# Reordering the gates at the end of a graph layer, with the residual base on VectorE

## Chip, core and metric

The kernel runs on one core of a Trainium2 chip. A core has TensorE (PE, matrix products into eight PSUM banks), VectorE (DVE), ScalarE (ACT), GpSimd (POOL) and SyncE (SP, which issues loads here). The metric is the device time of one execution in microseconds, the median of several.

## What is computed

Four layers are added one after another to x, 256 nodes by 512 features: a graph diffusion, a mixture of experts with feed-forward experts, a second graph layer, and a mixture of LSTM experts. The change is in the third, cut here to what matters (h is the normalised x):

```python
m = relu(concat(h[src], edge_attr) @ W1.T + b1) @ W2.T + b2
agg = segment_sum(m, dst)
i_r, i_z, i_n = split(agg @ W_ih.T + b_ih)
h_r, h_z, h_n = split(h @ W_hh.T + b_hh)
r, z = sigmoid(i_r + h_r), sigmoid(i_z + h_z)
n = tanh(i_n + r * h_n)
h_new = (1 - z) * n + z * h
x = x + h + gamma * (h_new - run_mean) * rsqrt(run_var + eps) + beta
```

There are 4352 edges, so the edge part is a loop of 34 tiles of 128 edges.

## The kernel before

The nodes are two tiles of 128 rows (n = 0, 1). A float32 product is made of three matmuls of split operands: `hi*hi + hi*lo + lo*hi`. Weights come in chunks of 512x512: SyncE loads one into `raw`, ScalarE rounds it to `whi` (L565), VectorE subtracts to `wlo` (L791). Each of the three engines has its own written order of instructions, and `cut_to(q)` in the orders of ScalarE and VectorE says up to which chunk the splits are to be done there. A split waits for the slot that it writes; a load waits for the VectorE split of the chunk four before it.

The order of the second graph layer: TensorE makes the first linear part, then the recurrent products of the reset gate (g = 0, banks 6 and 7) and of the update gate (g = 1, banks 2 and 3) for both tiles (`whh`). ScalarE copies all four to `gh` (`gh_copy`). Then the edge loop runs: GpSimd gathers rows (L541), TensorE makes the edge products (L1293 to L1295, into banks 2 to 5), VectorE adds (L1232, `mp`), ScalarE cuts (L757), VectorE splits (L1212, `m_lo`) and writes one-hot tiles (L1219), and TensorE sums by destination (L1641, L1643, banks 0 and 1). VectorE also splits the edge attributes for four tiles at a time (L1203, `ea_lo`). Behind its last gather GpSimd makes the base of the residual, x + g2b + xn, in place (L547 and L548, for both tiles), where g2b and g2s are the shift and scale of the batch normalisation.

After the loop: the recurrent products of the candidate (g = 2, banks 4 and 5), the aggregate through W2, its split, and the input products `Wih`. TensorE takes these tile by tile, in each the reset, update and candidate gate. VectorE's loop (L1257 on) goes tile by tile too: it adds the two parts of each gate (L1260), takes the sigmoids from ScalarE (L775), multiplies the reset gate in (L1266), builds the residual (L1270 to L1273), adds the candidate (L1276), takes the tanh (L777) and finishes x (L1279, L1280). `link(...)` marks an instruction whose successor on VectorE waits for its end by a semaphore; without it the next may start behind it.

Behind the layer come the layer norm of x (L808 to L818, its root on GpSimd, L471), the transposes of the normalised x on TensorE (L1322), the routing logits (L1407), the routing on VectorE (L944 to L972, among them the cast L951) and the LSTM experts. `keep_busy` (L1314) gives TensorE matmuls without use between two stages. While the logits are made, ScalarE copies the transposes (L584), cuts a chunk and writes two cuts more (L702, L705), and GpSimd subtracts for the low rows of the biases (L488).

Of the kernel before, what the change touches and what calls it, by code (L numbers as in the profile page):

```python
# [27 lines left out]
NT = T // P  # L28
D = 512
KB = D // P  # L30
# [8 lines left out]
SPL = 4  # L39
# [34 lines left out]
CHUNK = {key: n for n, key in enumerate(ORDER)}  # L74
# [13 lines left out]
def build(nc, A, out, node_rows):  # L88
    f32, f32r, bf16, i32, u32 = (mybir.dt.float32, mybir.dt.float32r, mybir.dt.bfloat16,
                                 mybir.dt.int32, mybir.dt.uint32)  # L90
    ALU = mybir.AluOpType
    ACT = mybir.ActivationFunctionType
# [3 lines left out]
    with ctx:  # L96
# [8 lines left out]
        whi = [sb(f"whi{i}", [P, KB, C], f32r) for i in range(SPL)]  # L105
        wlo = [sb(f"wlo{i}", [P, KB, C], f32r) for i in range(SPL)]
        x = sb("x", [P, NT, D])
        xn = sb("xn", [P, NT, D])
# [102 lines left out]
        with ExitStack() as st:  # L211
            g1_xT_hi = sb("g1_xT_hi", [P, NT, KB, P], f32r, st)
            g1_xT_lo = sb("g1_xT_lo", [P, NT, KB, P], f32r, st)
            A_sb = sb("A_sb", [P, NT, D], f32, st)
            gh = sb("gh", [P, NT, 3, D], f32, st)
# [4 lines left out]
            gsel = sb("gsel", [P, 3, P], f32r, st)  # L220
# [14 lines left out]
            with ExitStack() as st2:  # L235
# [5 lines left out]
                rz = sb("rz", [P, NT, 3, D], f32, st2)  # L241
# [3 lines left out]
            g2s = sb("g2s", [P, D], f32, st)  # L245
            g2b = sb("g2b", [P, D], f32, st)
# [7 lines left out]
        B = [ctx.enter_context(nc.psum_tensor(f"bank{i}", [P, C], f32)) for i in range(8)]  # L254
# [62 lines left out]
        def both_tiles(eng, n, first_tile, value, chunk):  # L317


            if n == 0:  # L320
                eng.wait_ge(first_tile, value)
            else:
                eng.wait_ge(chunk_used, chunk + 1)


        class Run:
# [61 lines left out]
            "a_ps", "a_sb", "a_out", "gh_ps", "gh_sb", "w1e_hi", "w1e_lo", "ea_hi", "ea_lo", "e_ps",  # L388
            "mp", "m_hi", "m_lo", "hot", "sum_ps", "s1_hi", "s1_lo", "agg_ps", "agg", "ag_hi", "ag_lo",
            "deg_d", "deg_ps", "ones", "warm",  # L390
            "gi_ps", "rz_in", "rz", "n_in", "n", "rows", "gsel", "x_base")}
        ea_in = [sem(f"g1_ea_in{i}") for i in range(3)]
        gath_in = [sem(f"g1_gath_in{i}") for i in range(GATH)]
        out_done = sem("out_done")
# [63 lines left out]
        def _(pool):  # L458
# [15 lines left out]
            bn_link = Chain(pool, pool_chain)  # L474
# [46 lines left out]
            for r in range(4):  # L521
# [7 lines left out]
                out=mp[:, SUMS - 1, :], out_offset=None, in_=A["x"],  # L529
# [12 lines left out]
                    out=gath[:, t % GATH, :], out_offset=None, in_=node_rows[:, :],  # L542
                    in_offset=bass.IndirectOffsetOnAxis(ap=src_i[:, t:t + 1], axis=0)).then_inc(gath_in[t % GATH], 16)


            for n in range(NT):
                bn_link(pool.tensor_tensor(x[:, n, :], x[:, n, :], g2b[:, :], ALU.add))  # L547
                pool.tensor_tensor(x[:, n, :], x[:, n, :], xn[:, n, :], ALU.add).then_inc(g1["x_base"], 1)  # L548

            root(3)  # L550
            moe_params(A["lstm_b"], A["L1_ffn_bo"])
# [4 lines left out]
        def _(act):  # L556
# [19 lines left out]
            def cut_to(n):  # L576
                while done[0] < n:
                    cut_hi(done[0])
                    done[0] += 1
# [164 lines left out]
            def gh_copy(g, n):  # L744
                both_tiles(act, n, g1["gh_ps"], g + 1, CHUNK[("gnn", "Whh", g)])
                act.activation(gh[:, n, g, :], B[(6, 2, 4)[g] + n][:, :], ACT.Copy).then_inc(g1["gh_sb"], 1)

            for g in range(2):
                for n in range(NT):
                    gh_copy(g, n)  # L750
                if g == 0:
                    cut_to(first + SPL + 1)
            for t in range(ET):
                act.wait_ge(g1["mp"], t + 1)
                if t >= MSG:
# [14 lines left out]
            cut_to(first + 2 * SPL)  # L770
            cut_to(first + 2 * SPL + 1)
            for n in range(NT):
                for g in range(2):
                    act.wait_ge(g1["rz_in"], 2 * n + g + 1)
                    act.activation(rz[:, n, g, :], rz[:, n, g, :], ACT.Sigmoid).then_inc(g1["rz"], 1)  # L775
                act.wait_ge(g1["n_in"], n + 1)
                act.activation(rz[:, n, 2, :], rz[:, n, 2, :], ACT.Tanh).then_inc(g1["n"], 1)  # L777
            cut_to(first + 2 * SPL + 3)
# [7 lines left out]
        def _(dve):  # L786
# [14 lines left out]
            def cut_to(n):  # L801
                while done[0] < n:
                    cut_lo(done[0])
                    done[0] += 1
# [450 lines left out]
                                  ag_hi[:, 2 * b:2 * b + 2, :].bitcast(f32), ALU.subtract).then_inc(g1["ag_lo"], 1)  # L1255
            cut_to(first + 2 * SPL)
            for n in range(NT):  # L1257
                for g in range(2):
                    both_tiles(dve, n, g1["gi_ps"], g + 1, CHUNK[("gnn", "Wih", g)])
                    dve.tensor_tensor(rz[:, n, g, :], B[2 * g + n][:, :], gh[:, n, g, :], ALU.add)\  # L1260
                       .then_inc(g1["rz_in"], 1)
                    if n == 0 and g == 0:
                        cut_to(first + 2 * SPL + 1)
                dve.wait_ge(g1["rz"], 2 * n + 1)
                dve.wait_ge(g1["gh_sb"], 2 * NT + n + 1)
                link(dve.tensor_tensor(rz[:, n, 0, :], rz[:, n, 0, :], gh[:, n, 2, :], ALU.mult))  # L1266

                dve.wait_ge(g1["rz"], 2 * n + 2)
                dve.wait_ge(g1["x_base"], n + 1)
                link(dve.tensor_tensor(gh[:, n, 0, :], rz[:, n, 1, :], xn[:, n, :], ALU.mult))  # L1270
                link(dve.tensor_tensor(gh[:, n, 0, :], gh[:, n, 0, :], g2s[:, :], ALU.mult))
                link(dve.tensor_tensor(x[:, n, :], x[:, n, :], gh[:, n, 0, :], ALU.add))
                link(dve.scalar_tensor_tensor(out=gh[:, n, 1, :], in0=rz[:, n, 1, :], scalar=1.0,  # L1273
                                              in1=g2s[:, :], op0=ALU.subtract, op1=ALU.mult))
                both_tiles(dve, n, g1["gi_ps"], 3, CHUNK[("gnn", "Wih", 2)])
                dve.tensor_tensor(rz[:, n, 2, :], rz[:, n, 0, :], B[4 + n][:, :], ALU.add)\  # L1276
                   .then_inc(g1["n_in"], 1)
                dve.wait_ge(g1["n"], n + 1)
                link(dve.tensor_tensor(rz[:, n, 2, :], rz[:, n, 2, :], gh[:, n, 1, :], ALU.mult))  # L1279
                link(dve.tensor_tensor(x[:, n, :], x[:, n, :], rz[:, n, 2, :], ALU.subtract))  # L1280
                if n == 0:
                    dve.bn_stats(stats[:, n, :], x[:, n, :])
            dve.drain().then_inc(layer_done, 1)
# [5 lines left out]

        @block.tensor  # L1290
        def _(pe):
            def mm3(ps, xh, xl, wh, wl, first, last):
                pe.matmul(ps, xh, wh, start=first, stop=False)  # L1293
                pe.matmul(ps, xh, wl, start=False, stop=False)
                return pe.matmul(ps, xl, wh, start=False, stop=last)  # L1295

            def product(ps, xh, xl, w, blocks, lo_ready, first, last):

# [10 lines left out]
            def has_chunk(n):  # L1309
                pe.wait_ge(lo_cut, n + 1)  # L1310

            def keep_busy(bank, n):
                for _ in range(n):
                    pe.matmul(bank[:, :].rearrange("p (k t) -> p k t", k=2), iota_b[:, 0:P],  # L1314
                              iota_b[:, :].unsqueeze(1).to_broadcast([P, 2, T]), start=True, stop=True)
# [284 lines left out]
            def whh(g, n):  # L1600
                q = CHUNK[("gnn", "Whh", g)]
                has_chunk(q)
                ps = B[(6, 2, 4)[g] + n]
                if g == 1:
                    pe.wait_ge(g1["a_sb"], n + 1)
                for k in range(KB):
                    mm3(ps[:, :], g1_xT_hi[:, n, k, :], g1_xT_lo[:, n, k, :],
                        whi[q % SPL][:, k, :], wlo[q % SPL][:, k, :], k == 0, False)
                pe.wait_ge(g1["rows"], 2)
                ins = pe.matmul(ps[:, :], gsel[:, 0 if g < 2 else 1, :], gb_rows[:, g * D:(g + 1) * D],  # L1610
                                start=False, stop=True)
                if n == 0:
                    ins.then_inc(g1["gh_ps"], 1)
                else:

                    ins.then_inc(chunk_used, 2 if g == 2 else 1)
# [7 lines left out]
            def edge_product(t):  # L1624
                g, j = t // GRP, t % GRP
                if j == 0:
                    pe.wait_ge(g1["ea_lo"], g + 1)
                if t >= EBANKS:
                    pe.wait_ge(g1["mp"], t - EBANKS + 1)
                elif t == 0:  # L1630
                    pe.wait_ge(g1["gh_sb"], 2 * NT)
                mm3(B[2 + t % EBANKS][:, :], ea_hi[:, g % 2, j * P:(j + 1) * P],
                    ea_lo[:, g % 2, j * P:(j + 1) * P], w1e_hi[:, :], w1e_lo[:, :], True, True)\
                    .then_inc(g1["e_ps"], 1)
# [33 lines left out]
            whh(2, 1)  # L1668
            pe.wait_ge(g1["ag_hi"], 2)
            pe.wait_ge(g1["ag_lo"], 2)  # L1670
            for n in range(NT):
                for g in range(3):
                    q = CHUNK[("gnn", "Wih", g)]
                    has_chunk(q)
                    ps = B[2 * g + n]
                    if g == 2:
                        pe.wait_ge(g1["gh_sb"], 2 * NT + n + 1)
                        pe.matmul(ps[:, :], gsel[:, 2, :], gb_rows[:, g * D:(g + 1) * D], start=True, stop=False)
                    for k in range(KB):
                        ins = mm3(ps[:, :], ag_hi[:, k, n * P:(n + 1) * P], ag_lo[:, k, n * P:(n + 1) * P],  # L1680
                                  whi[q % SPL][:, k, :], wlo[q % SPL][:, k, :], g < 2 and k == 0, k == KB - 1)
                    ins.then_inc(g1["gi_ps"] if n == 0 else chunk_used, 1)

            keep_busy(B[6], 30)
            pe.wait_ge(layer_done, 3)
            gating(2)
            experts(lstm)
# [61 lines left out]
```

## Time and profile before

| | |
|---|---|
| median of 3 runs | 534.62 us (532.62 to 535.49) |
| the profiled execution | 529.06 us, span from first to last instruction 527.3 us |
| granted TensorE clock, mean | 0.952 |
| busy: PE, PEld, DVE | 472.8, 373.7, 420.9 us |
| busy: ACT, POOL | 285.9, 178.8 us |

PE is the matmuls, PEld the loads of their stationary operand. A matmul's end is modelled, so from one start to the next tells more than the duration. The idle time in brackets is that of the engine just ahead of the instruction, with what ended it. The edge loop lies from about 240 to 300 us, the gates from 312 to 336, the gating of the last layer from 336 to 353 us.

### The profile page before, as it was taken

The numbers are of one execution on the slowest core, as the hardware profiler recorded it, in microseconds if no ns is written. First come the engines' busy times: TensorE is split into PE (matmuls) and PEld (weight loads), VectorE is DVE, ScalarE is ACT, GpSimd is POOL, SyncE is SP. The second block draws the span as 40 slices with busy tenths as digits, with TensorE's granted clock in tenths as the row PEclk, the third lists the DMA queues.
The fourth block names the chain that finished last, engine by engine and source line by source line (L and its number), as shares of the span: only waits on it lengthen the run. The fifth ranks groups of instructions, "written<-read, shape, count | busy, mean of one in ns | idle before, by whom it ended". The sixth has DMA issues, their size and how long they took to land. (4 is left out here: it accounts for less than half of the span.)

```text
span 527.3 us, 6322 instructions
## 1 busy us (share of the span) xinstructions
PE 472.8 (90%) x2317; PEld 373.7 (71%) x2317; DVE 420.9 (80%) x654; ACT 285.9 (54%) x305; POOL 178.8 (34%) x90
## 2 busy tenths in 40 slices
PE   4889599999999998798999799779699999999883
PEld 2555368888888785586899688357478888887662
DVE  6988775979889773887999769875699898868572
ACT  3154255767677664523444353535477777848361
POOL 4601999999920000557787200220000000000000
PEclk9899689999999999799999999959799999999998
DMA  8910624786878628558676044042658778764601
GB/s 305 269 56 9 231 80 160 281 307 241 305 292 303 250 99 324 192 216 253 211 233 198 2 160 159 10 159 80 239 173 325 300 288 310 260 259 162 237 2 41
DMA packets 18612, 105.24 MB, mean 200 GB/s; under 512 B 3008, under 2 KB 3168, under 8 KB 7696
## 3 DMA queue, kind: packets, MB, share of 16 engines
q1 hardware_dynamic: 14080, 92.41, 47.1%
q0 software_dynamic: 4208, 12.32, 8.2%
q8 instruction: 22, 0.36, 0.3%
q14 instruction: 14, 0.11, 0.1%
q10 hardware_dynamic: 288, 0.03, 0.0%
HBM read 103.71 MB, written 1.05 MB: 199 GB/s over the span
## 5 line engine op out<-in xcount | busy, mean ns | idle before, releaser
L791 DVE TENSOR_TENSOR wlo<-raw,whi 128x2048 fp32r<-128x2048 f32 x73 | 168.7, 2332 | 23.3 <-ACT whi L565 22.0
L565 ACT ACTIVATE whi<-raw 128x2048 fp32r<-128x2048 f32 x73 | 137.4, 1911 | 5.9 <-DMA raw<-in_weights_dram 5.9
L516 POOL TENSOR_TENSOR g2v<-g2v,minus_half 128x512 f32<-128x512 f32 x1 | 82.0, 81970 | 0.1
L1300 PE MATMUL bank<-whi,xe_hi 128*128 128x512 f32 x192 | 78.7, 410 | 2.0 <-DVE wlo L796 1.2
L1301 PE MATMUL bank<-wlo,xe_hi 128*128 128x512 f32 x192 | 76.3, 397 | 0.0
L1305 PE MATMUL bank<-whi,xe_lo 128*128 128x512 f32 x192 | 52.5, 395 | 0.0
L541 POOL DMA_INDIRECT gath<-node_rows,src_i x34 | 45.5, 1338 | 14.2 <-DVE mp L1232 8.9
L471 POOL TENSOR_TENSOR rstd<-var_eps,minus_half 128x2 f32<-128x2 f32 x4 | 3.0, 738 | 136.6 <-DVE var_eps L813 136.6
L1300 PE MATMUL bank<-whi,hT_hi 128*128 128x512 f32 x112 | 45.0, 402 | 2.1 <-ACT hT_hi L610 2.1
L1300 PEld LDWEIGHTS bank<-whi,xe_hi 128*128 128x128 f32 x192 | 37.0, 192 | 10.9 <-issue 1.6
L1301 PE MATMUL bank<-wlo,hT_hi 128*128 128x512 f32 x112 | 44.4, 397 | 0.0
L1305 PEld LDWEIGHTS bank<-whi,xe_lo 128*128 128x128 f32 x192 | 36.1, 188 | 8.7
L1301 PEld LDWEIGHTS bank<-wlo,xe_hi 128*128 128x128 f32 x192 | 36.8, 192 | 7.6
L757 ACT ACTIVATE m_hi<-mp 128x512 fp32r<-128x512 f32 x34 | 21.5, 633 | 34.2 <-DVE mp L1232 29.5
L621 ACT ACTIVATE act<-bank 128x512 f32<-128x512 f32 x30 | 17.9, 598 | 32.0 <-PE bank L1495 32.0
L1641 PE MATMUL bank<-onehot,m_hi 128*128 128x256 f32 x136 | 33.5, 281 | 1.3 <-DVE m_lo L1212 1.3
L1643 PE MATMUL bank<-onehot,m_lo 128*128 128x256 f32 x136 | 33.3, 280 | 0.0
L1314 PE MATMUL bank<-iota_b 128*128 128x512 bf16 x121 | 31.0, 401 | 0.0
L1305 PE MATMUL bank<-whi,hT_lo 128*128 128x512 f32 x112 | 30.7, 395 | 0.0
L604 ACT ACTIVATE y_hi<-bank,wslot 128x512 fp32r<-128x512 f32 x19 | 13.1, 687 | 32.2 <-PE bank L1305 32.2
L796 DVE TENSOR_TENSOR wlo<-raw,whi 128x2048 fp32r<-128x2048 f32 x12 | 26.9, 2287 | 2.9 <-ACT whi L571 2.8
L1641 PEld LDWEIGHTS bank<-onehot,m_hi 128*128 128x128 f32 x136 | 25.6, 188 | 3.1 <-DVE m_lo L1212 1.7
(297 smaller groups left out, 994.1 us busy)
## 6 DMA issues: line engine op xcount, KB each, us to landing
raw<-in_weights_dram SPq DMA_DIRECT2D x85, 1024.0 KB, 4.9
ea<-in_ea_dram SPq DMA_DIRECT2D x8, 256.0 KB, 3.1
gath<-node_rows,src_i POOLq DMA_INDIRECT x34, 3.8
x<-in_x_dram SPq DMA_DIRECT2D x1, 512.0 KB, 4.0
gw<-in_L_ffn_gw_dram POOLq DMA_DIRECT2D x1, 512.0 KB, 6.4
node_rows<-A_sb POOLq DMA_DIRECT2D x2, 256.0 KB, 2.9
out_dram<-x SPq DMA_DIRECT2D x1, 512.0 KB, 2.8
g_b<-in_L_gnn_b_dram POOLq DMA_DIRECT2D x1, 256.0 KB, 7.4
```

The costliest lines, as they stand in the source:

```text
L516: bn_link(pool.tensor_tensor(g2v[:, :], g2v[:, :], minus_half[:, 0:1].to_broadcast([P, D]), ALU.pow))
L541: pool.indirect_dma_start(out=gath[:, t % GATH, :], out_offset=None, in_=node_rows[:, :], in_offset=bass.IndirectOffsetOnAxis(ap=src_i[:, ...
L565: act.activation(whi[n % SPL][:, :, :], raw[n % RAW][:, :, :], ACT.Copy).then_inc(hi_cut, 1)
L757: act.activation(m_hi[:, t % MSG, :], mp[:, t % SUMS, :], ACT.Relu).then_inc(g1["m_hi"], 1)
L791: dve.tensor_tensor(wlo[n % SPL][:, :, :], raw[n % RAW][:, :, :], whi[n % SPL][:, :, :].bitcast(f32), ALU.subtract).then_inc(lo_cut, 1)
L796: dve.tensor_tensor(wlo[q % SPL][:, :, :], raw[q % RAW][:, :, :], whi[q % SPL][:, :, :].bitcast(f32), ALU.subtract).then_inc(run.more_lo, 1)
L1300: pe.matmul(ps, xh[:, blocks + k, :], whi[w % SPL][:, k, :], start=first and k == 0, stop=False)
L1301: pe.matmul(ps, xh[:, blocks + k, :], wlo[w % SPL][:, k, :], start=False, stop=False)
L1305: ins = pe.matmul(ps, xl[:, blocks + k, :], whi[w % SPL][:, k, :], start=False, stop=last and k == KB - 1)
L1314: pe.matmul(bank[:, :].rearrange("p (k t) -> p k t", k=2), iota_b[:, 0:P], iota_b[:, :].unsqueeze(1).to_broadcast([P, 2, T]), start=True, ...
L1641: pe.matmul(ps, m_hi[:, t % MSG, k * P:(k + 1) * P], onehot[:, t % HOT1, :], start=t == 0 and k % 2 == 0, stop=False, skip_group_check=True)
L1643: ins = pe.matmul(ps, m_lo[:, t % MSG, k * P:(k + 1) * P], onehot[:, t % HOT1, :], start=False, stop=t == ET - 1, skip_group_check=True)
```

## The change

In words: the recurrent reset products stay in banks 6 and 7 through the edge loop, and the input reset products are added to them there, so that ScalarE takes the reset sigmoid straight from the bank; two copies and two additions go. TensorE makes the input products gate by gate, in each for both tiles. The update gate's sigmoid is taken of the negated sum, so it gives 1 - z =: u, and x is made from (x + xn*g2s + xn + g2b) - u*xn*g2s + u*g2s*n. The base of that is made on VectorE, four instructions per tile ahead of the split of the first LSTM chunk, and GpSimd's four instructions go. The warming matmuls behind the products become 16 instead of 30, in another bank.

```diff
@@ GpSimd
-            for n in range(NT):
-                bn_link(pool.tensor_tensor(x[:, n, :], x[:, n, :], g2b[:, :], ALU.add))
-                pool.tensor_tensor(x[:, n, :], x[:, n, :], xn[:, n, :], ALU.add).then_inc(g1["x_base"], 1)
@@ ScalarE
-            for g in range(2):
-                for n in range(NT):
-                    gh_copy(g, n)
-                if g == 0:
-                    cut_to(first + SPL + 1)
+            both_tiles(act, 1, None, 0, CHUNK[("gnn", "Whh", 0)])
+            cut_to(first + SPL + 1)
+            for n in range(NT):
+                gh_copy(1, n)
...
             for n in range(NT):
-                for g in range(2):
-                    act.wait_ge(g1["rz_in"], 2 * n + g + 1)
-                    act.activation(rz[:, n, g, :], rz[:, n, g, :], ACT.Sigmoid).then_inc(g1["rz"], 1)
+                both_tiles(act, n, g1["gi_ps"], 1, CHUNK[("gnn", "Wih", 0)])
+                act.activation(rz[:, n, 0, :], B[6 + n][:, :], ACT.Sigmoid).then_inc(g1["r"], 1)
+            for n in range(NT):
+                act.wait_ge(g1["z_in"], n + 1)
+                act.activation(rz[:, n, 1, :], rz[:, n, 1, :], ACT.Sigmoid, scale=-1.0).then_inc(g1["u"], 1)
+            for n in range(NT):
                 act.wait_ge(g1["n_in"], n + 1)
                 act.activation(rz[:, n, 2, :], rz[:, n, 2, :], ACT.Tanh).then_inc(g1["n"], 1)
@@ VectorE
             cut_to(first + 2 * SPL)
             for n in range(NT):
-                for g in range(2):
-                    both_tiles(dve, n, g1["gi_ps"], g + 1, CHUNK[("gnn", "Wih", g)])
-                    dve.tensor_tensor(rz[:, n, g, :], B[2 * g + n][:, :], gh[:, n, g, :], ALU.add)\
-                       .then_inc(g1["rz_in"], 1)
-                    if n == 0 and g == 0:
-                        cut_to(first + 2 * SPL + 1)
-                dve.wait_ge(g1["rz"], 2 * n + 1)
-                dve.wait_ge(g1["gh_sb"], 2 * NT + n + 1)
-                link(dve.tensor_tensor(rz[:, n, 0, :], rz[:, n, 0, :], gh[:, n, 2, :], ALU.mult))
-
-                dve.wait_ge(g1["rz"], 2 * n + 2)
-                dve.wait_ge(g1["x_base"], n + 1)
-                link(dve.tensor_tensor(gh[:, n, 0, :], rz[:, n, 1, :], xn[:, n, :], ALU.mult))
-                link(dve.tensor_tensor(gh[:, n, 0, :], gh[:, n, 0, :], g2s[:, :], ALU.mult))
+                link(dve.tensor_tensor(gh[:, n, 0, :], xn[:, n, :], g2s[:, :], ALU.mult))
+                dve.tensor_tensor(A_sb[:, n, :], xn[:, n, :], g2b[:, :], ALU.add)
                 link(dve.tensor_tensor(x[:, n, :], x[:, n, :], gh[:, n, 0, :], ALU.add))
-                link(dve.scalar_tensor_tensor(out=gh[:, n, 1, :], in0=rz[:, n, 1, :], scalar=1.0,
-                                              in1=g2s[:, :], op0=ALU.subtract, op1=ALU.mult))
+                link(dve.tensor_tensor(x[:, n, :], x[:, n, :], A_sb[:, n, :], ALU.add))
+            cut_to(first + 2 * SPL + 1)
+            for n in range(NT):
+                dve.wait_ge(g1["r"], n + 1)
+                dve.wait_ge(g1["gh_sb"], NT + n + 1)
+                ins = dve.tensor_tensor(rz[:, n, 0, :], rz[:, n, 0, :], gh[:, n, 2, :], ALU.mult)
+            link(ins)
+            for n in range(NT):
+                both_tiles(dve, n, g1["gi_ps"], 2, CHUNK[("gnn", "Wih", 1)])
+                dve.tensor_tensor(rz[:, n, 1, :], B[2 + n][:, :], gh[:, n, 1, :], ALU.add)\
+                   .then_inc(g1["z_in"], 1)
+            for n in range(NT):
+                dve.wait_ge(g1["u"], n + 1)
+                link(dve.tensor_tensor(gh[:, n, 0, :], gh[:, n, 0, :], rz[:, n, 1, :], ALU.mult))
+                dve.tensor_tensor(gh[:, n, 1, :], rz[:, n, 1, :], g2s[:, :], ALU.mult)
+                link(dve.tensor_tensor(x[:, n, :], x[:, n, :], gh[:, n, 0, :], ALU.subtract))
+            for n in range(NT):
                 both_tiles(dve, n, g1["gi_ps"], 3, CHUNK[("gnn", "Wih", 2)])
                 dve.tensor_tensor(rz[:, n, 2, :], rz[:, n, 0, :], B[4 + n][:, :], ALU.add)\
                    .then_inc(g1["n_in"], 1)
                 dve.wait_ge(g1["n"], n + 1)
                 link(dve.tensor_tensor(rz[:, n, 2, :], rz[:, n, 2, :], gh[:, n, 1, :], ALU.mult))
-                link(dve.tensor_tensor(x[:, n, :], x[:, n, :], rz[:, n, 2, :], ALU.subtract))
+                link(dve.tensor_tensor(x[:, n, :], x[:, n, :], rz[:, n, 2, :], ALU.add))
                 if n == 0:
                     dve.bn_stats(stats[:, n, :], x[:, n, :])
@@ TensorE (whh: the reset group is left open; edge loop: waits for two copies, not four)
-            for n in range(NT):
-                for g in range(3):
-                    q = CHUNK[("gnn", "Wih", g)]
-                    has_chunk(q)
-                    ps = B[2 * g + n]
+            for g in range(3):
+                q = CHUNK[("gnn", "Wih", g)]
+                has_chunk(q)
+                for n in range(NT):
+                    ps = B[(6, 2, 4)[g] + n]
...
-            keep_busy(B[6], 30)
+            keep_busy(B[0], 16)
```

## Rows read from the trace of the kernel before

**Rows 1.** The page: the chain that ended last, by engine.
```profile
PE 29%; DVE 6%; ACT 2%; issue 1%; POOL 0%; DVEq 0%; ACTq 0%
```

**Rows 2.** The chain in order of time: start us, us, what.
```profile
322.22 0.70 DVE gh L1271
...
322.94 0.70 DVE x L1272
...
325.12 0.64 ACT rz L777
```

**Rows 3.** Timeline of VectorE, the gates: start us, us, engine, line, operation [idle before].
```profile
315.05 2.29 DVE L791 TENSOR_TENSOR wlo<-raw,whi 128x2048 fp32r<-128x2048 f32 x1 [3.20 <-ACT whi L565]
317.26 0.68 DVE L1260 TENSOR_TENSOR rz<-bank,gh 128x512 f32<-128x512 f32 x1
317.86 2.28 DVE L791 TENSOR_TENSOR wlo<-raw,whi 128x2048 fp32r<-128x2048 f32 x1
320.06 0.68 DVE L1260 TENSOR_TENSOR rz<-bank,gh 128x512 f32<-128x512 f32 x1
...
325.79 0.69 DVE L1279 TENSOR_TENSOR rz<-rz,gh 128x512 f32<-128x512 f32 x1 [0.70 <-ACT rz L777]
...
334.96 0.69 DVE L1280 TENSOR_TENSOR x<-x,rz 128x512 f32<-128x512 f32 x1
```

**Rows 4.** Timeline of TensorE: first input product, warming matmuls, transposes of the next layer.
```profile
312.41 0.39 PE L1293 MATMUL bank<-whi,ag_hi 128*128 128x512 f32 x1
...
329.75 6.65 PE L1314 MATMUL bank<-iota_b 128*128 128x512 bf16 x30
339.55 1.27 PE L1322 MATMUL bank<-eye,xn 128*128 128x128 f32 x8 [3.15 <-DVE xn L818]
```

**Rows 5.** Timeline of GpSimd, the base: first and last of four instructions.
```profile
287.94 1.32 POOL L547 TENSOR_TENSOR x<-x,g2b 128x512 f32<-128x512 f32 x1
...
292.34 1.59 POOL L548 TENSOR_TENSOR x<-x,xn 128x512 f32<-128x512 f32 x1
```

**Rows 6.** Timeline of VectorE, the last edge tiles: beside GpSimd's base, and after it.
```profile
287.89 1.93 DVE L1212 SCALAR_TENSOR_TENSOR m_lo<-mp,m_hi 128x512 fp32r<-128x512 f32 x1
289.74 1.38 DVE L1219 TENSOR_SCALAR onehot<-iota_t,dst_f 128x256 fp32r<-128x256 f32 x1
...
291.65 1.16 DVE L1212 SCALAR_TENSOR_TENSOR m_lo<-mp,m_hi 128x512 fp32r<-128x512 f32 x1
292.73 1.48 DVE L1203 TENSOR_TENSOR ea_lo<-ea,ea_hi 128x256 fp32r<-128x256 f32 x1
...
294.99 0.67 DVE L1212 SCALAR_TENSOR_TENSOR m_lo<-mp,m_hi 128x512 fp32r<-128x512 f32 x1
295.59 0.34 DVE L1219 TENSOR_SCALAR onehot<-iota_t,dst_f 128x256 fp32r<-128x256 f32 x1
295.86 0.68 DVE L1232 TENSOR_TENSOR mp<-bank,gath 128x512 f32<-128x512 f32 x1
```

**Rows 7.** Timeline of TensorE, the same stretch, and the first recurrent product after it.
```profile
290.90 0.28 PE L1641 MATMUL bank<-onehot,m_hi 128*128 128x256 f32 x1
291.01 0.27 PE L1643 MATMUL bank<-onehot,m_lo 128*128 128x256 f32 x1
294.26 0.50 PE L1293 MATMUL bank<-w1e_hi,ea_hi 128*128 128x512 f32 x1 [2.98 <-DVE ea_lo L1203]
...
300.60 0.39 PE L1293 MATMUL bank<-whi,g_xT_hi 128*128 128x512 f32 x1
```

**Rows 8.** Stretch of the transposes: busy time of each engine, granted clock, DMA, GB/s.
```profile
339.50:345.00 5.50, 5.46 (x26) 4.62 (x27) 5.39 (x8) 4.73 (x5) 1.58 (x3) 0.57 0.31 78
```

**Rows 9.** Timeline of TensorE: the transposes of an earlier layer, right behind warming matmuls.
```profile
47.53 1.06 PE L1322 MATMUL bank<-eye,xn 128*128 128x128 f32 x8
```

**Rows 10.** Timelines of GpSimd and VectorE, the gating: the bias rows and the cast.
```profile
345.65 3.41 POOL L488 TENSOR_TENSOR b_rows<-b_raw,b_rows 8x1536 fp32r<-8x1536 f32 x1 [4.57 <-ACT b_rows L705]
...
346.15 2.95 DVE L951 CAST topf<-topi 128x16 f32<-128x16 uint32 x1
```

More of the change, by code:

```diff
@@ L390, in build @@
             "deg_d", "deg_ps", "ones", "warm",
-            "gi_ps", "rz_in", "rz", "n_in", "n", "rows", "gsel", "x_base")}
+            "gi_ps", "z_in", "r", "u", "n_in", "n", "rows", "gsel")}
         ea_in = [sem(f"g1_ea_in{i}") for i in range(3)]
@@ L1291, in _, with mm3 @@
         def _(pe):
[L1292 to L1295, printed above, removed]
+            def mm3(ps, xh, xl, wh, wl, first, last, skip=False):
+                pe.matmul(ps, xh, wh, start=first, stop=False, skip_group_check=skip)
+                pe.matmul(ps, xh, wl, start=False, stop=False, skip_group_check=skip)
+                return pe.matmul(ps, xl, wh, start=False, stop=last, skip_group_check=skip)
             def product(ps, xh, xl, w, blocks, lo_ready, first, last):
@@ L1607, in whh @@
                     mm3(ps[:, :], g1_xT_hi[:, n, k, :], g1_xT_lo[:, n, k, :],
-                        whi[q % SPL][:, k, :], wlo[q % SPL][:, k, :], k == 0, False)
+                        whi[q % SPL][:, k, :], wlo[q % SPL][:, k, :], k == 0, False, skip=g == 0)
                 pe.wait_ge(g1["rows"], 2)
                 ins = pe.matmul(ps[:, :], gsel[:, 0 if g < 2 else 1, :], gb_rows[:, g * D:(g + 1) * D],
-                                start=False, stop=True)
+                                start=False, stop=g > 0, skip_group_check=g == 0)
                 if n == 0:
@@ L1630, in edge_product @@
                 elif t == 0:
-                    pe.wait_ge(g1["gh_sb"], 2 * NT)
+                    pe.wait_ge(g1["gh_sb"], NT)
                 mm3(B[2 + t % EBANKS][:, :], ea_hi[:, g % 2, j * P:(j + 1) * P],
@@ L1670, in _ @@
             pe.wait_ge(g1["ag_lo"], 2)
-            for n in range(NT):
-                for g in range(3):
-                    q = CHUNK[("gnn", "Wih", g)]
-                    has_chunk(q)
-                    ps = B[2 * g + n]
+            for g in range(3):
[3 more added lines that the diff above has]
+                    ps = B[(6, 2, 4)[g] + n]
                     if g == 2:
-                        pe.wait_ge(g1["gh_sb"], 2 * NT + n + 1)
+                        pe.wait_ge(g1["gh_sb"], NT + n + 1)
                         pe.matmul(ps[:, :], gsel[:, 2, :], gb_rows[:, g * D:(g + 1) * D], start=True, stop=False)
@@ L1680, in _ @@
                         ins = mm3(ps[:, :], ag_hi[:, k, n * P:(n + 1) * P], ag_lo[:, k, n * P:(n + 1) * P],
-                                  whi[q % SPL][:, k, :], wlo[q % SPL][:, k, :], g < 2 and k == 0, k == KB - 1)
+                                  whi[q % SPL][:, k, :], wlo[q % SPL][:, k, :], g == 1 and k == 0, k == KB - 1,
+                                  skip=g == 0)
                     ins.then_inc(g1["gi_ps"] if n == 0 else chunk_used, 1)
-            keep_busy(B[6], 30)
+            keep_busy(B[0], 16)
             pe.wait_ge(layer_done, 3)
```

## The prediction

> **What bounds the kernel now.** I read the page's chain line first: it follows the last work back and finds mostly TensorE [rows 1], but that is a mean over stages, so I went to the stages that the diff touches. The first is the end of the second graph layer. In order of time the chain there is VectorE from one linked instruction to the next, broken only by the two tanh of ScalarE [rows 2]. In VectorE's own timeline from 317.26 us to the last update of x at 334.96 there is hardly any idle time but for the two tanh [rows 3]. TensorE is not the bound there: it runs the input products from 312.41 to 329.75 us without a gap, then fills with 30 warming matmuls and stands still until the normalised rows come [rows 4]. So the layer's end is a list of VectorE instructions, and what counts is their number and price.
>
> The second stage is the edge loop before it, because the diff takes four instructions off GpSimd that run there. They lie between 287.94 and 293.93 us [rows 5]. In just that stretch four VectorE instructions on SBUF operands are long: 1.93 and 1.16 us where the same line takes 0.67, 1.38 where the same line takes 0.34, and 1.48 for half the columns of a split [rows 6]. Each ends about as long after a GpSimd instruction's end as it takes by itself: the engine waits for GpSimd. TensorE, gapless until then, has nothing running for 2.98 us before 294.26, which is put down to that last VectorE split [rows 7].
>
> **The change part by part.**
>
> Residual base off GpSimd. All four GpSimd instructions go [rows 5], and with them the cause of the stall. On VectorE the excess is 1.26 + 1.04 + 0.49 us and, against a whole split, at least 0.8: 3.6 us or more [rows 6]. Not all of it is on the path, for VectorE had some lead. What the path gets is TensorE's hole: the last matmul before it starts at 291.01 and its like are 0.12 apart, so the next was due at 291.13; it starts at 294.26, 3.1 us late [rows 7]. Is VectorE able to follow without GpSimd? Per edge tile TensorE needs three matmuls of 0.23 and eight of 0.12, 1.65 us; VectorE needs 0.60 for the sum, 0.60 for the split and 0.27 for the one-hot tile [rows 6], with 0.6 more in each fourth tile, 1.62 us. So TensorE sets the pace, and its work up to the recurrent product at 300.60 moves up. I take 3.1 us gained, bounds 2.5 (VectorE trails by some waits) and 3.6 (all of its excess). All that follows (sums, aggregate, splits, the recurrent products) is a chain that starts at this point and moves with it.
>
> Recurrent reset part kept in its banks. Two ScalarE copies before the edge loop go. The loop's first product waits for the copies of the update gate, which still stand last, so nothing is gained.
>
> Order of the gates on TensorE. 74 matmuls in 17.34 us are 0.234 each [rows 4]: reset of both tiles is done at 318.0, update at 320.8 and 323.7, candidate at 326.7 and 329.7, in the times of the trace of before. All are earlier than VectorE will ask for them (below), so the order itself is worth nothing. The reset sigmoids run on ScalarE meanwhile, some 7 us before they are wanted.
>
> VectorE's list. Two linked instructions start 0.72 to 0.73 us apart [rows 2]; after one without a link the next starts 0.60 later [rows 6]. A weight split takes 2.20 from start to start [rows 3]. From 317.26 on, in the times of before, the new list is:
> base, per tile three linked and one free, 2 x (3 x 0.725 + 0.60) = 5.55;
> weight split 2.20;
> reset times candidate part, 0.60 + 0.73 = 1.33;
> update adds, 2 x 0.60, and about 0.15 until the first sigmoid (0.68 add, 0.64 sigmoid, 0.04 between) is back = 1.35;
> per tile two linked and one free, 2 x 2.05 = 4.10;
> per tile the candidate: add 0.72, tanh 0.67, product 0.72, add 0.73, 2 x 2.84 = 5.68;
> statistics of the first tile 0.60.
> Together 20.8 us. The old list runs from 317.26 to 335.68 [rows 3], 18.4 us. So the tail gets 2.4 us longer. In counts: 24 elementwise instructions instead of 20, less the 0.12 us for each link given up. The candidate sums are wanted at 331.8 and 335.3 in this clock, after TensorE has them (326.7, 329.7): VectorE is still the bound. Bounds: 1.8 (every link that is given up also lets its successor overlap) to 3.0 (none does). VectorE waits 3.20 us for a weight chunk ahead of 315.05 [rows 3], and the eight base instructions would fit there, but they are written behind that split, so this hole stays. The Trainium skill, page "VectorE: DVE Perf Modes", section "The DRAIN you can't avoid", reports that a semaphore after each instruction costs nothing extra. Here the rows differ, 0.725 linked and 0.60 free; by the page the tail would be 0.6 us longer than I say.
>
> What the later split moves. The cut of the first LSTM chunk comes 5 us later on VectorE, so SyncE's load behind it (that of four chunks later) too. Behind it in SyncE's queue stand only loads that wait for splits after the layer. It is for the experts, which start only after the gating: 0.
>
> Warming matmuls, 16 instead of 30. Thirty take 6.65 us; sixteen end 3.1 us sooner. The products end 3.1 us sooner and the layer only 0.7 sooner, so the hole before the transposes grows from 3.15 us [rows 4] to 3.15 + 3.1 + 2.4 = 8.7 us. In before, the granted clock is 1.00 (2.4 GHz) in the hole and falls to half during the transposes, a mean of 0.57 from 339.5 to 345 [rows 8]. With the longer hole it has fallen before they begin. At the full clock eight transposes take 1.06 us [rows 9], here 1.27 [rows 4]; with each step doubled about 2.1. Behind them stand the copies of ScalarE, its cut and its two further copies, GpSimd's instruction and VectorE's cast. I take 0.6 us lost, bounds 0 and 0.9. From there on the clock was low anyway. The rule that speaks against the change is that of the Trainium skill, "TensorE: Matmul & The Clock Gate", section "Why this matters for your kernels": idle gaps between bursts of matmuls bring the engine back to half clock. The row at 339.5 agrees; taken alone the rule prices this part, with no gain against it, at the same 0.6 us.
>
> Sum: -3.1 + 2.4 + 0.6 = -0.1 us. The profiled execution took 529.06 us (span 527.3 and 1.8 around it); it becomes 529.0. The median of the runs is 534.62, 5.6 above; the parts changed don't scale with that, so I subtract the same: 534.5.
>
> **The rivals.**
>
> The relief isn't on the path (slower). If VectorE or the gathers hold the last edge tiles anyway once GpSimd is quiet, the 3.1 us don't come, and 2.4 + 0.6 stay: 537.6. It decides from the point where less than 0.4 us of the hole is recovered. Against it: the hole is the only long one in that stretch, and the gathers are issued before it. 12 in 100.
>
> The cast comes free (faster). Behind the layer VectorE's cast at 346.15 takes 2.95 us and ends with GpSimd's instruction of 345.65 to 349.06 [rows 10]. It is 0.5 us too late to start first. If the new timing shifts ScalarE's side by more than TensorE's, so that the cast starts ahead, 2.8 us go (2.95 less the 0.2 or so of so small an instruction): 531.7. Against it: both follow the same transposes, so their distance stays. 10 in 100.
>
> The list is cheaper than its count (faster). If the base instructions found the hole before 315.05, or the two tiles' chains overlapped more, the tail would cost nothing: 532.1. Against it: the written order. 4 in 100.
>
> The kept banks don't do their work. Were ScalarE to read the reset sums late, VectorE would wait at the reset product; it has 7 us of cover, so even then 534.5.
>
> **How the numbers follow.** My case has 66 in 100; with the scatter of three runs (532.62 to 535.49) that is faster 4, same 60, slower 2. About 0.5% (2.7 us) is what a measurement can tell from no change. The first rival's 12 are 10 slower and 2 same, the second's 10 are 9 faster and 1 same, the third's 4 are 2 and 2; 8 are left for what I don't see, 3 faster, 2 same, 3 slower. Faster 0.18, same 0.67, slower 0.15. Bounds of the terms: -3.6 + 1.8 + 0 = -1.8 and -2.5 + 3.0 + 0.9 = +1.4, with 1.4 us of scatter on either side, 531.4 to 537.4; the upper end goes to the slower rival, 537.6.
>
> **What would show it.** The VectorE instructions of the last edge tiles at 0.67 and 0.34 us, and TensorE's hole gone; the recurrent product some 3 us earlier. From the end of the split before the gates to the last update of x 20.8 us instead of 18.4, gapless but for 0.15 and two tanh. A half clock already at the transposes, which take some 2 us; the cast still near 2.9. I am wrong if the tail is no longer than before, if the edge loop ends less than 2 us earlier, or if the cast is short.

## The result, and the profile after

The changed kernel takes 531.0 us in the median of 20 runs, the kernel before 535.76 in 20 runs beside it. The ratio is 0.9925 with a 95% interval of 0.9896 to 0.9955: 4.0 us faster, between 2.4 and 5.6. This ratio and those below leave out executions more than 1.5% above the quickest of their kernel, here among others one of 677.11 us at a mean granted clock of 0.65; the quotient of the two medians is 0.9911. I had forecast -0.1 us, no change, and 534.5 us, with 531.4 as the lower end. So the change is faster, by 0.75% in the middle of the interval, a case to which I gave 18 in 100, and the median lies 0.4 us below my range.

The profiled execution took 530.8 us (span 529.0), which is longer than that of before (529.06). One execution of each is no comparison here, for both kernels scatter by some 10 us. The stages of the two traces can be compared. In that of after the edge loop up to the recurrent product is 3.0 us shorter, the gates 2.4 longer, the gating 0.7 longer, and the last layer 2.5 us longer, because the clock falls there near 499 us (last section). That last term is why its span is the longer one.

The first view is VectorE's timeline at the last edge tiles; it answers to [rows 6].

```profile
287.53 0.68 DVE L1210 SCALAR_TENSOR_TENSOR m_lo<-mp,m_hi 128x512 fp32r<-128x512 f32 x1
288.13 0.34 DVE L1217 TENSOR_SCALAR onehot<-iota_t,dst_f 128x256 fp32r<-128x256 f32 x1
...
289.06 0.68 DVE L1210 SCALAR_TENSOR_TENSOR m_lo<-mp,m_hi 128x512 fp32r<-128x512 f32 x1
289.66 0.42 DVE L1201 TENSOR_TENSOR ea_lo<-ea,ea_hi 128x256 fp32r<-128x256 f32 x1
```

With GpSimd quiet the same four instructions take 0.68, 0.34, 0.68 and 0.42 us instead of 1.93, 1.38, 1.16 and 1.48, 3.8 us less together. TensorE's timeline, which answers to [rows 7]:

```profile
290.84 0.40 PE L1294 MATMUL bank<-w1e_hi,ea_hi 128*128 128x512 f32 x1
...
292.49 0.40 PE L1294 MATMUL bank<-w1e_hi,ea_hi 128*128 128x512 f32 x1
...
296.98 0.40 PE L1294 MATMUL bank<-whi,g_xT_hi 128*128 128x512 f32 x1
```

The first row is the last group's edge product, which stood behind the hole of 2.98 us in before. There is no hole; one tile follows the other in 1.65 us, and from that product to the recurrent one it takes 6.14 us.

VectorE's list at the layer's end, which answers to [rows 3]:

```profile
311.43 2.29 DVE L789 TENSOR_TENSOR wlo<-raw,whi 128x2048 fp32r<-128x2048 f32 x1 [3.19 <-ACT whi L561]
313.64 0.68 DVE L1256 TENSOR_TENSOR gh<-xn,g2s 128x512 f32<-128x512 f32 x1
...
319.19 2.29 DVE L789 TENSOR_TENSOR wlo<-raw,whi 128x2048 fp32r<-128x2048 f32 x1
321.40 1.29 DVE L1264 TENSOR_TENSOR rz<-rz,gh 128x512 f32<-128x512 f32 x2
322.73 1.29 DVE L1268 TENSOR_TENSOR rz<-bank,gh 128x512 f32<-128x512 f32 x2
324.11 0.69 DVE L1272 TENSOR_TENSOR gh<-gh,rz 128x512 f32<-128x512 f32 x1
...
329.61 0.69 DVE L1280 TENSOR_TENSOR rz<-rz,gh 128x512 f32<-128x512 f32 x1 [0.70 <-ACT rz L775]
...
333.76 0.69 DVE L1281 TENSOR_TENSOR x<-x,rz 128x512 f32<-128x512 f32 x1
```

From 313.64 to the last update (333.76, and 0.72 to its successor) it is 20.8 us, as forecast, 2.4 more than before. The wait of 3.19 us ahead of the split stays. TensorE behind it, which answers to [rows 4], and two stretches of the granted clock (the figure ahead of the last two), which answer to [rows 8]:

```profile
326.13 3.63 PE L1315 MATMUL bank<-iota_b 128*128 128x512 bf16 x16
338.36 1.94 PE L1323 MATMUL bank<-eye,xn 128*128 128x128 f32 x8 [8.60 <-DVE xn L816]
```

```profile
334.00:338.00 4.00, 0.00 (x0) 0.00 (x0) 2.94 (x6) 2.60 (x2) 2.06 (x2) 0.50 0.00 0
338.30:344.50 6.20, 6.14 (x27) 5.31 (x28) 5.40 (x8) 4.76 (x5) 1.57 (x3) 0.50 0.39 119
```

The hole is 8.60 us, the clock is at half before the transposes begin, and they take 1.94 us instead of 1.27. The cast still meets GpSimd, as in [rows 10]; the timelines of GpSimd and of VectorE:

```profile
345.13 3.41 POOL L488 TENSOR_TENSOR b_rows<-b_raw,b_rows 8x1536 fp32r<-8x1536 f32 x1 [5.25 <-ACT b_rows L701]
```
```profile
345.63 2.94 DVE L949 CAST topf<-topi 128x16 f32<-128x16 uint32 x1
```

So all that I had named came, close to its price. What I hadn't named is what the experiments look for.

### The profile page after: what moved, and what is told of

Its sections match the earlier page's. It is cut to its first block, busy times and chain, and to the rows that moved or that the text cites. A ratio compares the mean times of both kernels' runs of the same rounds, so it can differ in the third digit from the quotient of the medians.

```text
span 529.0 us, 6291 instructions
## 1 busy us (share of the span) xinstructions
PE 474.4 (90%) x2303; PEld 375.4 (71%) x2303; DVE 420.0 (79%) x658; ACT 284.6 (54%) x303; POOL 172.8 (33%) x86
## 4 chain that ended last, share of the span: by engine, by line
PE 73%; DVE 19%; ACT 3%; issue 3%; DMA 1%; POOL 1%; DVEq 0%; ACTq 0%; POOLq 0%
PE bank L1301 14%; PE bank L1302 14%; PE bank L1306 14%; DVE wlo L789 4%; PE bank L1294 3%; PE bank L1644 3%; PE bank L1642 3%; PE bank L1296 2%; PE bank L1295 2%; PE bank L1528 2%; PE bank L1496 2%; PE bank L1453 2%; PE bank L1505 2%; PE bank L1454 2%; PE bank L1507 2%
## 5 line engine op out<-in xcount | busy, mean ns | idle before, releaser
L1302 PE MATMUL bank<-wlo,xe_hi 128*128 128x512 f32 x192 | 77.5, 403 | 0.0
L1302 PE MATMUL bank<-wlo,hT_hi 128*128 128x512 f32 x112 | 45.5, 406 | 0.0
L1315 PE MATMUL bank<-iota_b 128*128 128x512 bf16 x107 | 27.9, 404 | 0.0
```

The lines of the kernel that those rows point to most:

```text
L1302: pe.matmul(ps, xh[:, blocks + k, :], wlo[w % SPL][:, k, :], start=False, stop=False)
```

## The experiments

The theory is that the change's gain is TensorE's hole in the edge loop, and that the hole costs more than its 3.1 us because in some executions the granted clock falls to half in it. The rival is that the gain lies in the gates' new order or in the tail. Nine kernels ran, and the kernel before three more times. A trace is one profiled execution. This table puts the stages of the traces side by side, in us, from the timelines: the stretch from the restart behind the hole to the recurrent product (for kernels without the hole, the same product); from the first input product to the start of the last update of x; from the transposes to the gather (the first matmul of the gathering matrix G with the split xn).

| trace | restart to recurrent | input product to x | transposes to gather |
|---|---|---|---|
| before | 6.34 | 22.55 | 13.58 |
| before, second | 7.52 | 22.54 | 13.52 |
| before, third | 8.92 | 22.55 | 14.25 |
| before, fourth | 7.67 | 22.55 | 13.49 |
| after | 6.14 | 24.96 | 14.25 |
| e1, 30 warming matmuls | no hole | 24.96 | 14.26 |
| e2, base on GpSimd | 7.77 | 22.31 | 14.26 |
| e3, before with base on VectorE | no hole | 25.46 | 14.25 |
| e4, base early | no hole | 21.70 | 14.26 |
| e5, base on GpSimd late | no hole | 22.31 | 12.43 |
| e6, before with the hole filled | 6.35 | 22.54 | 12.61 |
| e7, bias rows late | no hole | 24.96 | 10.35 |
| e8, all three | no hole | 21.68 | 10.35 |
| e9, 52 warming matmuls | no hole | 24.95 | 13.50 |

**The kernel before again**, with no edit.

> The kernel before, unchanged: 1.000 of before. Its trace is a second look at the same program. The theory of the hole (the time came from TensorE's hole of 3 us in the edge loop, and from a half clock that starts in that hole in some executions) expects the same hole, and perhaps a granted clock of half from about 294 us on for 3 us or more; the rival (the time came from the order of the gates or the tail) expects no such thing.

Measured: 1.0011 [0.9977, 1.0044]. Its trace has the hole, and the clock falls in it. TensorE at the restart, and the stretches ahead of it and around it:

```profile
292.33 0.79 PE L1293 MATMUL bank<-w1e_hi,ea_hi 128*128 128x512 f32 x1 [3.15 <-DVE ea_lo L1203]
292.92 0.63 PE L1294 MATMUL bank<-w1e_lo,ea_hi 128*128 128x512 f32 x1
```
```profile
291.00:295.00 4.00, 2.67 (x9) 2.38 (x10) 3.99 (x7) 0.63 (x1) 0.99 (x1) 0.60 0.00 0
286.00:291.00 5.00, 3.18 (x22) 2.65 (x20) 5.00 (x6) 1.57 (x3) 4.82 (x5) 1.00 0.26 78
```

The clock is 1.00 until 291 us and 0.60 in the mean of the next four: the three edge products behind the hole start 0.59 and 0.43 us apart, instead of 0.34 and 0.23 in the first trace. In the profile that I predicted from it had stayed at 1.00. Two more traces:

> The kernel before, a third look. The hole of 3 us is there; whether the half clock starts in it is open (1 of 2 looks so far): with it the edge loop takes 62.2 us from its first sum to the recurrent product, without it 60.1.

> The kernel before, a fourth look, as the third: 62.2 us of edge loop with a half clock at the hole, 60.1 without.

Measured: 537.89 and 533.17 us, one execution each, and the half clock in both. The third trace has the longest restart; TensorE's timeline at the restart, and the stretch around it:

```profile
296.43 0.79 PE L1293 MATMUL bank<-w1e_hi,ea_hi 128*128 128x512 f32 x1 [2.96 <-DVE ea_lo L1203]
```
```profile
295.00:302.00 7.00, 5.57 (x20) 4.99 (x21) 5.29 (x9) 1.26 (x2) 1.09 (x1) 0.54 0.01 2
```

So the clock falls at this hole in three of four traces of before, and in the trace of e2 as well. Against 6.34 us with the clock at full the restart takes 1.2, 2.6, 1.3 and 1.4 us longer. Over all five traces that have the hole open it is 1.3 us in the mean. My expectation had numbers for the whole loop (62.2 and 60.1 us); it was 64.9 and 63.2 in the two, because another stall comes earlier in the loop (below).

**The base back on GpSimd.**

```diff
+            (GpSimd, behind the last gather)
+            for n in range(NT):
+                bn_link(pool.tensor_tensor(x[:, n, :], x[:, n, :], g2b[:, :], ALU.add))
+                pool.tensor_tensor(x[:, n, :], x[:, n, :], xn[:, n, :], ALU.add).then_inc(g1["x_base"], 1)
             (VectorE)
-                dve.tensor_tensor(A_sb[:, n, :], xn[:, n, :], g2b[:, :], ALU.add)
+                dve.wait_ge(g1["x_base"], n + 1)
                 link(dve.tensor_tensor(x[:, n, :], x[:, n, :], gh[:, n, 0, :], ALU.add))
-                link(dve.tensor_tensor(x[:, n, :], x[:, n, :], A_sb[:, n, :], ALU.add))
```

> The changed kernel, but the two adds of the residual base are again on GpSimd behind the last gather; VectorE has four instructions fewer in the tail, 2.65 us. Theory of the hole: VectorE's four long instructions and the 3 us hole of TensorE are back, so 3.1 lost and 2.65 gained against the changed kernel by the sum, and where a half clock starts in the hole more is lost: 0.995 to 1.001 of before. Rival (the gates' order is the gain): the hole costs nothing, 2.65 us better than the changed kernel, 0.987.

Measured: 0.9995 [0.9960, 1.0030]. The gain is gone although the tail is 2.65 us shorter (22.31 against 24.96) and the gates keep the new order. The rival's 0.987 lies outside. The four long VectorE instructions are back to within 0.01 us, and TensorE's hole is back with 2.89 us; two of the four, from VectorE's timeline:

```profile
290.95 1.93 DVE L1214 SCALAR_TENSOR_TENSOR m_lo<-mp,m_hi 128x512 fp32r<-128x512 f32 x1
292.81 1.37 DVE L1221 TENSOR_SCALAR onehot<-iota_t,dst_f 128x256 fp32r<-128x256 f32 x1
```

**Only the base moved**, the gates in their old order.

```diff
-            (GpSimd: the four instructions of the base)
+            (VectorE, ahead of the gates)
+            for n in range(NT):
+                link(dve.tensor_tensor(x[:, n, :], x[:, n, :], g2b[:, :], ALU.add))
+                link(dve.tensor_tensor(x[:, n, :], x[:, n, :], xn[:, n, :], ALU.add))
```

> The kernel before with the gates in their old order, and only the residual base moved to VectorE, four linked adds of 0.725 us ahead of the gates. Theory of the hole: -3.1 + 2.9 = -0.2 us by the sum, and the share that comes from the clock on top, up to -4 us: 0.992 to 1.000. Rival: the tail is 2.9 us longer and nothing comes back, 1.005.

Measured: 0.9938 [0.9897, 0.9980], 3.3 us faster. The tail is 2.9 us longer (25.46 against 22.55), as counted, and the kernel is faster all the same. This one edit gives what the whole change gives, within the intervals; the rest of the change can't be told from nothing.

**The hole filled, nothing else.** Twelve matmuls without use stand in TensorE's hole in the kernel before. GpSimd, VectorE and the delay stay.

```diff
+                if t == ET - 2:
+                    pe.wait_ge(g1["mp"], t - EBANKS + 1)
+                    keep_busy(B[2 + t % EBANKS], 12)
                 if j == 0:
                     pe.wait_ge(g1["ea_lo"], g + 1)
```

> The kernel before, base still on GpSimd, with 12 warming matmuls (2.7 us) put into TensorE's hole ahead of the last group's edge product. VectorE's long instructions and the 3.1 us of delay stay. If part of the change's gain is a half clock that starts in the hole (2.2 us in the second look at before), that part comes: 0.996 to 0.998 of before, and no fall of the clock between 286 and 300 us in its trace. If the delay itself is all, 1.000.

Measured: 0.9944 [0.9900, 0.9987], 3.0 us faster. TensorE's timeline and the clock around it:

```profile
292.37 2.77 PE L1314 MATMUL bank<-iota_b 128*128 128x512 bf16 x12
295.42 0.50 PE L1293 MATMUL bank<-w1e_hi,ea_hi 128*128 128x512 f32 x1 [0.28 <-DVE ea_lo L1203]
```
```profile
291.00:299.00 8.00, 7.72 (x47) 5.64 (x46) 7.87 (x11) 1.90 (x3) 4.01 (x3) 1.00 0.01 4
```

The edge product waits for VectorE as before, and the clock stays at 1.00. One trace with a full clock proves little, since the first of before has that too; the executions say more. The mean granted clock of all 12 is 0.954, that of the 23 of before beside them 0.947. The kernel is faster by work that computes nothing, and the clock is the only cause that the runs offer. The interval (0.7 to 5.3 us) holds the 1.3 us of the traces; its middle is higher.

**Warming matmuls, 30 and 52** instead of 16, in the changed kernel.

```diff
-            keep_busy(B[0], 16)
+            keep_busy(B[0], 30)        (e9: 52)
```

> The changed kernel with 30 warming matmuls behind the products again. The hole before the transposes shrinks from 8.6 to about 5.5 us. If the clock has then still fallen before the transposes they take 1.9 us and the time is that of the changed kernel, 0.992 of before; if it stays, they take 1.1 to 1.3 us and 0.6 us are gained, 0.991.

> The changed kernel with 52 warming matmuls (11.5 us) behind the products, so that TensorE works until just before the transposes. If the half clock at the transposes costs what I took, 0.6 us and more (the logits at full clock too, 1.5 us less, and the cast perhaps ahead of GpSimd): 0.6 to 2.8 us better than the changed kernel, 0.987 to 0.991 of before, transposes at 1.1 us. If the clock there is of no weight: 0.992.

Measured: 0.9890 [0.9850, 0.9930] and 0.9886 [0.9798, 0.9973], neither to be told from the 0.9925 of the change; the second stands for six executions only. With 30 the hole is 5.58 us and the transposes still take 1.94; with 52 they take 1.06 and the gather comes 0.75 us earlier. TensorE's timeline, e1 and then e9:

```profile
342.84 1.94 PE L1323 MATMUL bank<-eye,xn 128*128 128x128 f32 x8 [5.58 <-DVE xn L816]
```
```profile
338.50 1.06 PE L1323 MATMUL bank<-eye,xn 128*128 128x128 f32 x8 [0.82 <-DVE xn L816]
```

That sizes the term: 0.7 us, seen in the traces, too small for these intervals. In e9 GpSimd's instruction comes earlier by about as much, so the cast (3.31 us there) still meets it.

**The base early**, the eight VectorE instructions ahead of the split.

```diff
+            (the loop of four base instructions per tile)
             cut_to(first + 2 * SPL)
-            (the loop of four base instructions per tile)
```

> The changed kernel with the eight base instructions of VectorE ahead of the split before the gates, where VectorE waits 3.2 us for a chunk. 5.55 us of work, 3.2 of it in the hole: the layer ends 3.2 us earlier than in the changed kernel if VectorE is the bound of the tail, so 0.986 of before; if TensorE or a split holds the tail instead, no change, 0.992.

Measured: 0.9912 [0.9873, 0.9951], 528.53 us in the median. The tail is 3.26 us shorter in the trace, 21.70 against 24.96: the hole ahead of the split is used. The timing doesn't show it clearly; 0.986 is just outside the interval. VectorE's timeline, the first base instruction and the splits behind the last:

```profile
307.26 0.68 DVE L1255 TENSOR_TENSOR gh<-xn,g2s 128x512 f32<-128x512 f32 x1
...
312.82 4.50 DVE L789 TENSOR_TENSOR wlo<-raw,whi 128x2048 fp32r<-128x2048 f32 x2
```

**The base on GpSimd, but late**, behind the last split of the edge loop. The edit is that of e2 with a wait in front:

```diff
+            pool.wait_ge(g1["mp"], ET)
+            pool.wait_ge(g1["m_lo"], ET)
```

> The changed kernel with the base adds on GpSimd, but only behind the last split of the edge loop, where VectorE mostly waits. The theory of the hole expects no hole of TensorE, the tail 2.65 us shorter than in the changed kernel, at most one split of a chunk waiting for GpSimd's last instruction: 2 to 2.65 us better than the changed kernel, 0.987 of before. The rival (anything on GpSimd there costs as much as it saves) expects 0.992.

Measured: 0.9892 [0.9832, 0.9951], 527.24 us in the median of six executions. The interval holds 0.987 and 0.992, so the timing doesn't decide between the theory and the rival. In the trace the hole is gone and the tail is 2.65 us shorter. GpSimd's last instruction costs the first of two splits 0.96 us (5.45 for two instead of 4.49). GpSimd's timeline, then VectorE's at that place and in the gating:

```profile
300.18 1.29 POOL L550 TENSOR_TENSOR x<-x,xn 128x512 f32<-128x512 f32 x1
```
```profile
300.38 5.45 DVE L795 TENSOR_TENSOR wlo<-raw,whi 128x2048 fp32r<-128x2048 f32 x2 [0.94 <-ACT whi L567]
...
342.09 0.17 DVE L955 CAST topf<-topi 128x16 f32<-128x16 uint32 x1
...
342.95 4.33 DVE L941 TENSOR_TENSOR xn_lo<-xn,xn_hi 128x1024 fp32r<-128x1024 f32 x1
```

The last two rows show what my second rival described. In this trace the clock was back at full for the logits, VectorE came ahead of GpSimd's instruction at 342.73, and the cast took 0.17 us. But the next larger VectorE instruction met it instead and took 4.33 us instead of 1.22. The gather came 1.8 us earlier than in after, but 1.1 of that is the logits at the full clock: VectorE reads them 5.27 us behind the start of the transposes instead of 6.38. The trace of e6 has the cast free as well (0.17 us; 12.61 in the table), and there a small instruction four places on (L965) met GpSimd and took 3.45 us. e7 below has about the same clock and no meeting at all, and its gather comes 10.35 us behind the transposes, against 12.43 in e5 and 12.61 in e6. So my second rival's price was too high: the wait moves to a following instruction on SBUF operands, 2.1 to 2.3 us of it stay, and 0.5 to 0.7 are saved.

**The bias rows late**, on the changed kernel.

```diff
                 pool.wait_ge(gate["xn_cut"], 2 * nth)
+                if nth == 2:
+                    pool.wait_ge(gate["turner"], 2)
```

> The changed kernel with GpSimd's subtraction for the low bias rows waiting until the routing is done, so that it meets neither VectorE's cast nor its splits. If the 2.94 us of the cast lie on the path: 2.8 us better than the changed kernel, 0.987 of before, cast at 0.18 us. If TensorE's or ScalarE's work is as late anyway: 0.992.

Measured: 0.9935 [0.9893, 0.9977]. In the trace the gating is 3.9 us shorter (10.35 against 14.25) and the cast takes 0.17 us; the span is 524.0. Of the 3.9 us the edit explains 2.8, the cast; the other 1.1 are again the logits at the full clock, as in e5. This execution (525.82 us) is also the quickest of the twelve. The timing doesn't show the gain: 0.987 lies outside the interval. So one trace and 12 executions don't agree, and why the 2.8 us are missing in the timing stays open.

**All three** (e5's late base, e4's place for what is left of it on VectorE, e7's wait).

> The changed kernel with three edits: base adds on GpSimd behind the loop's last split, the rest of the base ahead of the split before the gates, and the bias rows late. By the sum 2.65 + 2.9 + 2.8 = 8.3 us better than the changed kernel, some 12 better than before: 0.977. If the pieces hide each other it stays above 0.983.

Measured: 0.9791 [0.9736, 0.9846], 523.15 us in the median of six executions, the fastest of all and clear of both kernels. The sum of the parts was 8.3 us against the changed kernel. In the trace it is 3.3 in the tail and 3.9 in the gating, of which 1.1 are the clock in the logits and not the edit. The tail is no shorter than e4's, because TensorE has become its bound. VectorE's timeline at the update adds:

```profile
317.15 0.69 DVE L1275 TENSOR_TENSOR rz<-bank,gh 128x512 f32<-128x512 f32 x1 [0.30 <-PE bank L1303]
319.89 0.69 DVE L1275 TENSOR_TENSOR rz<-bank,gh 128x512 f32<-128x512 f32 x1 [2.05 <-PE bank L1303]
```

VectorE waits 2.05 us for the second tile's update products. Of the traces with the new order only this one has the products of TensorE clearly on the path of the tail.

## Why the prediction was right or wrong

**What bounds the layer's end: right.** It is VectorE's list. It was counted as 20.8 us and is 20.8; the extra is 2.4 us, and the count holds for e2, e3 and e5 too (22.31, 25.46 and 22.31, each as its number of instructions says). Free instructions start 0.60 us behind one another and linked ones 0.72 in the changed kernel as well (313.64 to 314.36 linked, 314.36 to 314.96 free), so the rows stay 0.12 us apart. What the Trainium skill, "VectorE: DVE Perf Modes", section "The DRAIN you can't avoid", reports for a chain of eight copies, that the semaphore costs nothing extra, doesn't carry over to these instructions.

**The relief of the edge loop: right in place and, between the first two traces, in size.** TensorE's hole is gone, and from the first edge product to the recurrent one it is 58.05 us against 61.04, 3.0 less. What it lacked is the next point. My first rival, that the relief isn't on the path, fell: e2 loses what e3 gains.

**The missed term: the clock in the hole.** This is the step that failed. I priced the clock at the transposes, behind a hole of 3.15 us, and put it at nothing in the edge loop, behind a hole of 2.98. The trace of before had the clock at full there, and I took one execution for the rule. In three of four traces of before it is at half: 1.3 us in the mean of the traces that have the hole, 3.0 (0.7 to 5.3) by e6. Removing the hole removes that too. Two holes of about the same length in one trace, one with the fall and one without, should have told me that either may have it in the next execution.

**The clock at the transposes: right.** 0.6 forecast; 0.67 between the traces (14.25 against 13.58), 0.75 by e9. The rule that I quoted against the change (the Trainium skill, "TensorE: Matmul & The Clock Gate", section "Why this matters for your kernels": idle gaps bring the engine back to half clock) agrees with the hole before the transposes in every trace of before, and with that of the edge loop in three of four. It speaks for the change at the one where I hadn't applied it.

**The cast: right for the changed kernel**, 2.94 us. With GpSimd's instruction where it was, it comes free in two traces (e5, e6), whose logits ran at the full clock behind transposes at half; that saves 0.5 to 0.7 us and not the 2.8 of my rival.

**The sum.** With the missed term it is -3.1 - 1.3 + 2.4 + 0.7 = -1.3 us by the traces. Measured is -4.0 (-5.6 to -2.4), so between 1 and 4 us are missing by the traces. The timings price the hole higher, and three ways of reading them agree. e3 gains 3.3 us with a tail 2.9 longer, so its hole was worth 6.2; e2 is 3.7 us slower than the change with a tail 2.65 shorter, 6.4; e6's 3.0 and the delay of 3.1 make 6.1. Each of these is uncertain by 2 to 2.5 us. With 6.2 the sum is -3.1 us, inside the measured interval. So the timings leave nothing unexplained that is clear of noise; that the few traces show only 4.4 of the 6.2 us stays open.

One candidate for the rest is an early stall of the edge loop. In several traces of kernels of both kinds (n2, e6, e3, e1, e2) TensorE stands still near 251 us, and in e1 and e2 the clock falls there (0.50 from 252.3 to 259.0 us in e1). The change takes two ScalarE copies away just ahead of that stretch. But the traces don't show that this helps: from the first edge product to that of the last group, with the delay of the hole taken out, it is 53.2 us in the mean of six traces with four copies (51.6 to 54.2) and 53.2 in eight with two (51.9 to 56.8).

**The range.** It had the scatter of three runs at 1.4 us on either side. The 20 runs of before lie between 529.3 and 540.6, so the profiled execution at 529.06 was quicker than all of them: its trace has neither the half clock in the hole, nor the early stall, nor the fall in the last layer, and so its sum had no term for what the change takes from the others.

## What to carry to other kernels

VectorE work on SBUF operands and GpSimd arithmetic side by side cost VectorE a good part of what GpSimd takes (here 3.8 us beside four adds of 5.9 us together); put GpSimd's adds where VectorE waits for something else, not where it is one of two engines in step. In a kernel like this each hole of TensorE of about 3 us is to be priced twice, once for its length and once for a half clock behind it, whatever the one trace at hand shows, and a few matmuls without use inside it settle which part is which. When an engine's instruction list is shortened, look for which engine waits next (here TensorE, after 3.3 us).

## What the runs showed of the hardware

The granted clock falls at the same hole in some executions of the same program and not in others (three of four traces of before), and behind it the restart took 1.2 to 2.6 us longer. In the last layer the same thing happens at a smaller hole: in every trace TensorE is idle for 1.58 us there (at 498.5 in after, at 498.1 in before), and for 0.69 us a little later. The clock falls behind it in 7 of 14 traces, and from the first expert product to the end it is then 172.1 to 173.1 us, otherwise 169.6 to 169.9. The fall is in one of the five traces of before and e6, and in six of the nine others; that may be a cost of the change, but the traces are too few to say.

Such falls make a good part of the scatter of 10 us. The third trace of before has a span 8.8 us longer than the first: 2.4 in the edge loop up to the hole (the early stall), 2.6 behind the hole, 0.7 in the gating and 3.4 in the last layer; all but the first of these go with a half clock that the first trace doesn't have or has later.

VectorE waits for GpSimd by who started first, one whole instruction at a time: the split of 1.22 us took 4.33 when it began 0.22 us behind GpSimd's of 3.46 us. How close it goes is seen in e5 and e6: the same small instruction started within 0.02 us of GpSimd's in both, and took 0.17 us in e5 and 3.45 in e6. The add `mp`, which has one operand in a bank, was not lengthened: in e2 it took 0.68 us at 294.10 while GpSimd's add ran from 293.99 to 295.31.
